# A graph-network kernel: one pipeline of node groups from the attention mix to the first maximum table, and ScalarE copies the carries

## The chip, the cores and the metric

The kernel runs on one core of a Trainium2 chip. The metric is the time of one execution in device microseconds (us), the median over runs. Engines are TensorE (PE in the rows, PEld for its weight loads), VectorE (DVE), ScalarE (ACT), GpSimd (POOL) and SyncE (SP), which here only issues DMAs.

## What is computed

Four graph layers over 6250 nodes of 96 features and 200,000 edges sorted by target node, each added to its input and normalised. The part around the change is the first layer and its two norms:

```
edge_index = stack([src, dst])
h = (x @ W).reshape(N, 4, 24)                       # attention, with a self loop per node
e = leaky_relu(a_src[src] + a_dst[dst], 0.2);  e = exp(e - segment_max(e, dst)[dst])
out = segment_sum(e / segment_sum(e)[dst] * h[src], dst) + gat_bias
proj = out @ proj_W.T + proj_b
z = x + proj
L0 = ln_g * norm(z) + ln_b                          # first norm
x = layernorm(x + L0)                               # second norm
x = layernorm(x + L1(x))                            # two maximum convolutions: segment_max(x[src] @ W_msg + edge_attr @ W_edge) ...
x = layernorm(x + L2(x));  x = layernorm(x + L3(x)) # two means, three GCN sums
```

## The kernel before

Nodes are padded to 49 blocks of 128, and handled in 7 groups (`NG`) of 7 blocks (`GB`). Edges lie in 128 partitions, each with a run of consecutive edges. The program is written by hand, engine by engine: each engine runs its own list of instructions in order, and semaphores (`wait_ge`, `then_inc`) are the only links. A group of rows is 128 x 672 numbers (7 blocks of 96), with the extra columns of attention 700 or 728.

The three passes over the edges (attention, and two maximum passes) are alike. GpSimd gathers the rows of the source nodes from a table in device memory (L449, one gather for 128 edges, a ring of 4 slots), VectorE scans them in place, ScalarE stores the running result to `hist`. When a pass is through, GpSimd gathers each node's last running result into `EG` (L506, 49 gathers, one semaphore `end_gathered[g]` a group). GpSimd then waits for all seven stores of the next table (`table_stored`) before it gathers for the next pass.

Behind the attention pass, which is where the change lies, the order before is:

1. **Carries.** What runs from one partition's edges into the next is worked out for each node: TensorE multiplies the selector matrix with the carry rows in three bf16 parts (L783, 21 products a group, in PSUM `psO`), VectorE copies a group to `CQ` (`ARENA`, L1596). One buffer, so that the two take turns, seven times. Then VectorE sets a bias row (L1223) and makes the self-loop logits.
2. **Mix and projection, group by group.** VectorE makes the logits' differences (L1745 to L1751), ScalarE their exponentials (L982), VectorE mixes three sources and divides (L1756 to L1760). TensorE transposes the seven blocks (L660), ScalarE copies them out with a bias (L884), TensorE multiplies by the projection and adds `X` through an identity product (L668 and L671, 14 products), ScalarE copies the result into `C` (L1027), VectorE takes its moments (`bn_stats`, L1176).
3. **First norm.** The statistics of all 49 blocks are finished together (`squares(slice(0, NB))`, one square root, `scales_of(slice(0, NB))`): no group is normalised before the last group has been projected.
4. **Second norm and first maximum table, group by group.** ScalarE normalises `C` (L1001), VectorE multiplies and adds into `X` and takes moments, ScalarE takes the square root (L995) and normalises `X` (L1001), TensorE transposes (L660) and multiplies (L668 with 192 columns), VectorE copies half to the table `TB` (`take_rows`, L1203) which SyncE stores, ScalarE the other half to `R` (L892).

ScalarE's functions come in table sets: exponential and square root are in different ones, and an `ACT_TABLE_LOAD` stands in its program where the set changes.

Of the kernel before, what the change touches and what calls it, by code (L numbers as in the profile page):

```python
# [83 lines left out]

def out_group_base(phase, kind):

    n = 0
    for f in range(9):
        if f == phase and kind == "rows":
            return n  # L90
        n += NG
# [7 lines left out]
def build(nc, x, src, dst, dst_before, src_tiles, dst_tiles, edge_attr, att_W, att_src, att_dst, gat_bias, proj_WT, proj_b, ln_g, ln_b,  # L99
# [176 lines left out]
    psM = [psA, psB, psX]  # L276
    step_sums = [psA[:, 0:CW], psB[:, 0:CW], psX[:, 512:512 + CW]]
# [86 lines left out]
    normed = sem("normed")  # L364
    sqrt_in = sem("sqrt_in")
# [277 lines left out]
    def _(pe):  # L643
        def node_phase(f):

            cols = PHASE_COLS[f]
            base = out_group_base(f, "rows")

            rowsrc = X if f in (ATT, MAX1, MEAN1, GCN1) else C if f in (PROJ, MAX2) else EGW
            bias = f in (PROJ, MAX1, MAX2, MEAN1, MEAN2)  # L650
# [12 lines left out]
            def multiply_group(g):  # L663

                pe.wait_ge(xt_copied, f * NG + g + 1)
                pe.wait_ge(out_used, g + (base + 1))
                for k in range(GB):
                    mm = pe.matmul(OUTG[:, k, 0:cols], XT[0:depth, g % 2, k * P:(k + 1) * P], WR[0:depth, f, 0:cols],  # L668
                                   start=True, stop=f != PROJ)
                    if f == PROJ:  # L670
                        mm = pe.matmul(OUTG[:, k, 0:cols], ident[:, :], X[:, g * GB + k, :], start=False, stop=True)  # L671
# [4 lines left out]
            if f == PROJ:  # L676
                for g in range(NG):
                    transpose_group(g)
                    multiply_group(g)
                return  # L680
            transpose_group(0)
            for g in range(NG):
                if g + 1 < NG:
                    transpose_group(g + 1)
                multiply_group(g)

# [72 lines left out]
        def carries(f, q):  # L759
# [17 lines left out]
            base = out_group_base(f, "carry")  # L777
            with pe.Fori(0, NG) as g:
# [70 lines left out]
        node_phase(PROJ)  # L849
        for f in (MAX1, MAX2, MEAN1, MEAN2, GCN1, GCN2, GCN3):  # L850
            q = PASS_OF_PHASE[f]
            node_phase(f)
# [24 lines left out]
    def _(act):  # L877
        def rows_transposed(f, g):

            act.wait_ge(transposed, f * NG + g + 1)  # L880
            if g >= 2:
                act.wait_ge(out_ready, out_group_base(f, "rows") + g - 1)
            if f == PROJ:
                nc.scalar.activation(XT[0:DIM, g % 2, :], psX[0:DIM, 0:GB * P], ACT.Identity,  # L884
                                     bias=gbT[:, 0:1]).then_inc(xt_copied, 1)
            else:
                nc.scalar.copy(XT[0:DIM, g % 2, :], psX[0:DIM, 0:GB * P]).then_inc(xt_copied, 1)
# [136 lines left out]
        def projected_rows(g):  # L1024

            act.wait_ge(out_ready, out_group_base(PROJ, "rows") + g + 1)
            nc.scalar.copy(C[:, g * GB:(g + 1) * GB, :], OUTG[:, :, 0:DIM]).then_inc(out_used, 1)  # L1027
# [5 lines left out]
        exp_of_group(0)  # L1033
        for g in range(NG):
            if g + 1 < NG:
                exp_of_group(g + 1)
            rows_transposed(PROJ, g)
            projected_rows(g)
# [4 lines left out]
        for g in range(NG + 2):  # L1043
            if g < NG:
                deviations(slice(g * GB, (g + 1) * GB))
            if g + 2 < NG:
                normalise(C, g + 2, normed)
            if g < NG:
                act.wait_ge(scales_known, g + 2)
                normalise(X, g, rows_ready)  # L1050
            if 1 <= g < NG + 1:
                rows_transposed(MAX1, g - 1)
            if g >= 2:
                root_rows(MAX1, g - 2)
# [33 lines left out]
    def _(dve):  # L1088
# [461 lines left out]
        def carries(f, q):  # L1550
# [28 lines left out]
            else:  # L1579
# [8 lines left out]
                small_sent()  # L1588
            start = steps[0]
            with dve.Fori(0, NG) as g:  # L1590
# [4 lines left out]
                if q == 0:  # L1595
                    link(ts(CQ[:, here, :], OUTG[:, :, 0:W0], 1.0, None, ALU.mult))  # L1596
                else:
                    link(tt(C[:, here, :], OUTG[:, :, 0:DIM],
                            cpen[:, here].unsqueeze(2).broadcast_to([P, GB, DIM]), ALU.add))
# [131 lines left out]
        def projected_halves(g):  # L1731

            dve.wait_ge(out_used, out_group_base(PROJ, "rows") + g + 2)
            for b in range(g * GB, (g + 1) * GB):
                step(halves_of(C, b))

        for r in range(RING):
            dve.wait_ge(hist_stored[r], 16 * LAPS)
        link(tt(zself[:, :, :], TB0[:, :, SW:W0], ADN[:, :, :], ALU.add))
        link(stt(zself[:, :, :], zself[:, :, :], 0.2, zself[:, :, :], ALU.mult, ALU.max))  # L1740
        link(tt(CQ[:, :, SW:W0], CQ[:, :, SW:W0], per(cpen[:, :], NB, HEADS), ALU.add))
        for g in range(NG):
            here = slice(g * GB, (g + 1) * GB)
            dve.wait_ge(end_gathered[g], 16 * GB)
# [7 lines left out]
            dve.sem_inc(exp_in, 1)  # L1752
            dve.wait_ge(exp_done, 2 * ITERS + 3 + g)
# [9 lines left out]
            dve.sem_inc(rows_ready, 1)  # L1763
            if g:
                projected_halves(g - 1)
        projected_halves(NG - 1)
        dve.wait_ge(dve_step, steps[0])
        squares(slice(0, NB))
        scales_of(slice(0, NB))
        for g in range(NG):  # L1770
# [4 lines left out]
            for b in range(g * GB, (g + 1) * GB):  # L1775
                step(halves_of(X, b))
            dve.wait_ge(dve_step, steps[0])
            squares(here)
            if g >= 3:
                take_rows(MAX1, g - 3)  # L1780
            scales_of(here)
        for g in range(NG - 3, NG):
            take_rows(MAX1, g)
# [70 lines left out]
```

## Time and profile before

| | before |
|---|---|
| median of 3 runs | 8222.67 us (8220.35 to 8223.56) |
| profiled execution | 8213.33 us, span of its instructions 8211.5 us |
| mean granted TensorE clock | 0.642 of full speed |
| busy over the span | PE 52%, DVE 67%, ACT 18%, POOL 60% |

The span is that of one profiled execution. Times in rows count from its start. The stretch that the change touches reaches from about 2184 to 2360 us.

### The profile page before, as it was taken

The numbers are of one execution on the slowest core, as the hardware profiler recorded it, in microseconds if no ns is written. First come the engines' busy times: TensorE is split into PE (matmuls) and PEld (weight loads), VectorE is DVE, ScalarE is ACT, GpSimd is POOL, SyncE is SP. The second block draws the span as 40 slices with busy tenths as digits, with TensorE's granted clock in tenths as the row PEclk, the third lists the DMA queues.
The fourth block names the chain that finished last, engine by engine and source line by source line (L and its number), as shares of the span: only waits on it lengthen the run. The fifth ranks groups of instructions, "written<-read, shape, count | busy, mean of one in ns | idle before, by whom it ended". The sixth has DMA issues, their size and how long they took to land.

```text
span 8211.5 us, 69615 instructions
## 1 busy us (share of the span) xinstructions
PE 4235.5 (52%) x19184; PEld 2465.7 (30%) x19184; DVE 5538.0 (67%) x13229; ACT 1494.4 (18%) x2140; POOL 4891.3 (60%) x5030
## 2 busy tenths in 40 slices
PE   2100000000155655656555555556565498999999
PEld 1000000000131111111113111111111298999999
DVE  4765555555578888888886888888888775222222
ACT  0222222222231121111111111111211200010000
POOL 6777777777637777777776777777777600000000
PEclk6555555555566565565655555565555599999999
DMA  5333333333224444444443444444444275766767
GB/s 145 86 93 86 85 86 85 86 85 86 66 86 130 129 129 132 131 130 130 129 130 103 129 130 132 130 130 129 130 131 131 80 263 201 267 225 227 268 220 247
DMA packets 642303, 1132.83 MB, mean 138 GB/s; under 512 B 164860, under 2 KB 422287, under 8 KB 641634
## 3 DMA queue, kind: packets, MB, share of 16 engines
q1 hardware_dynamic: 360256, 440.38, 16.7%
q0 software_dynamic: 159184, 251.10, 15.5%
q10 hardware_dynamic: 122578, 438.40, 13.4%
q14 instruction: 210, 1.72, 0.1%
q8 instruction: 75, 1.23, 0.1%
HBM read 716.67 MB, written 412.70 MB: 138 GB/s over the span
## 4 chain that ended last, share of the span: by engine, by line
POOL 57%; PE 20%; issue 18%; DVE 3%; ACT 1%; DMA 1%; DVEq 0%; POOLq 0%; ACTq 0%; SPq 0%
POOL CG L449 55%; PE psB L723 6%; PE psX L723 6%; PE psA L723 6%; PE psO L668 1%; POOL ad_starts L461 1%; POOL EG L506 1%; ACT X L1001 1%; POOL EG L441 0%; PE psX L660 0%; PE psO L783 0%; DVE BUF L1120 0%; DVE EG L1172 0%; PE psO L671 0%; DVE halves L1176 0%
## 5 line engine op out<-in xcount | busy, mean ns | idle before, releaser
L449 POOL DMA_INDIRECT CG<-table,BUF x4704 | 4532.5, 964 | 1564.2 <-issue 1432.1
L695 PE MATMUL psO<-WE,BUF 128*128 128x384 f32 x1568 | 1137.3, 880 | 106.8 <-DMA BUF<-in_edge_attr 99.8
L766 PE MATMUL psA<-ident,F 128*100 128x128 f32 x1 | 0.5, 452 | 1740.0 <-DVEq L1404 1740.0
L475 POOL CAST CG<-EG x35 | 26.9, 769 | 1297.9 <-DVEq L1173 1297.9
L953 ACT COPY psX<-BUF 128x384 f32<-128x384 f32 x392 | 189.0, 482 | 3210.7 <-DVE STG L1531 1618.2
L695 PEld LDWEIGHTS psO<-WE,BUF 128*128 128x128 f32 x1568 | 460.6, 324 | 619.4 <-DMA BUF<-in_edge_attr 371.6
L1429 DVE TENSOR_TENSOR terms<-CG,ARENA 128x32 f32<-128x32 f32 x196 | 45.1, 230 | 792.5 <-DMA CG<-table,BUF 792.0
L1493 DVE TENSOR_SCALAR BUF<-iota,EG 128x392 bf16<-128x392 f16 x1568 | 542.3, 346 | 0.0
L766 PEld LDWEIGHTS psA<-ident,F 128*100 128x100 f32 x1 | 0.2, 158 | 1740.3 <-DVEq L1404 1740.3
L702 PE MATMUL psB<-BUF 128*128 128x392 bf16 x523 | 251.2, 480 | 511.4 <-DVE BUF L1499 511.2
L702 PE MATMUL psA<-BUF 128*128 128x392 bf16 x523 | 252.1, 482 | 506.4 <-DVE BUF L1499 506.4
L723 PE MATMUL psA<-CG,BUF 128*128 128x288 bf16 x4018 | 509.9, 287 | 6.2 <-DMA BUF<-counts 6.2
L723 PE MATMUL psB<-CG,BUF 128*128 128x288 bf16 x4018 | 509.2, 287 | 7.1 <-DMA BUF<-counts 7.1
L702 PE MATMUL psX<-BUF 128*128 128x392 bf16 x522 | 251.4, 482 | 504.6 <-DVE BUF L1499 504.6
L1490 DVE TENSOR_SCALAR BUF<-iota,EG 128x128 bf16<-128x128 f16 x1568 | 496.4, 317 | 20.6 <-DMA EG<-step_rows 20.6
L723 PE MATMUL psX<-CG,BUF 128*128 128x288 bf16 x3969 | 500.8, 286 | 0.6 <-POOL CG L478 0.6
L723 PEld LDWEIGHTS psA<-CG,BUF 128*128 128x128 bf16 x4018 | 495.4, 142 | 9.5 <-POOL CG L478 6.7
L723 PEld LDWEIGHTS psB<-CG,BUF 128*128 128x128 bf16 x4018 | 495.1, 142 | 9.8 <-issue 7.5
L1499 DVE TENSOR_SCALAR BUF<-iota,EG 128x392 bf16<-128x392 f16 x1568 | 495.9, 316 | 0.0
L723 PEld LDWEIGHTS psX<-CG,BUF 128*128 128x128 bf16 x3969 | 488.3, 142 | 1.6 <-POOL CG L478 0.8
L1524 DVE TENSOR_TENSOR XTQ<-CG,psO 128x768 f32<-128x768 f32 x196 | 288.6, 1473 | 216.5 <-DMA CG<-table,BUF 216.3
L1524 DVE TENSOR_TENSOR STG<-CG,psO 128x768 f32<-128x768 f32 x196 | 288.8, 1473 | 207.4 <-DMA CG<-table,BUF 206.8
(279 smaller groups left out, 7912.3 us busy)
## 6 DMA issues: line engine op xcount, KB each, us to landing
BUF<-counts SPq DMA_DIRECT2D x245, 784.0 KB, 5.8
BUF<-counts ACTq DMA_DIRECT2D x245, 784.0 KB, 6.2
counts<-BUF SPq DMA_DIRECT2D x1572, 98.0 KB, 2.4
hist<-CG ACTq DMA_DIRECT2D x392, 384.0 KB, 2.5
hist<-CG ACTq DMA_DIRECT2D x196, 416.0 KB, 2.6
CG<-table,BUF POOLq DMA_INDIRECT x4704
BUF<-in_edge_attr SPq DMA_DIRECT2D x392, 128.0 KB
table<-TB SPq DMA_DIRECT2D x14, 336.0 KB, 2.6
```

The source lines that it names most:

```text
L449: pool.indirect_dma_start(out=rows_in[:, u % RING, k, :], out_offset=None, in_=tab, in_offset=bass.IndirectOffsetOnAxis(ap=SRC[:, u * S + ...
L461: pool.indirect_dma_start(out=ad_starts, out_offset=bass.IndirectOffsetOnAxis(ap=start_i[:, b:b + 1], axis=0), in_=ADN[:, b, :], in_offset ...
L506: pool.indirect_dma_start(out=EG[:, b * width:(b + 1) * width], out_offset=None, in_=rec, in_offset=bass.IndirectOffsetOnAxis(ap=last_i[:, ...
L668: mm = pe.matmul(OUTG[:, k, 0:cols], XT[0:depth, g % 2, k * P:(k + 1) * P], WR[0:depth, f, 0:cols], start=True, stop=f != PROJ)
L695: mm = pe.matmul(ETERM[:, s, a, 0:4 * DIM], EA[:, s, a, :], WE[:, m, :, :].rearrange("k c d -> k (c d)"), start=True, stop=True)
L702: pe.matmul(sums, LO[:, j, 0, :], RHS[:, j, 0, :], start=True, stop=False)
L723: mm = pe.matmul(sums[:, 0:3 * DIM], CNT16[:, B % 3, b:b + NB * (P - 1) + 1:NB], PARTS[:, b, :], start=b == 0, stop=b == NB - 1, skip_grou ...
L953: nc.scalar.copy(reset_cols[:, :, 1:K9], reset[:, u * S:(u + 1) * S].unsqueeze(1).broadcast_to([P, DIM // 2, S])).then_inc(resets_ready, 1)
L1490: ts(LO[:, j, 0, :], iota16[:, 0:P], STEP[:, 2, n:n + 1], None, ALU.is_equal)
L1493: ts(RHS[:, j, 0, :], iota16[:, :], STEP[:, 0, n:n + 1], None, ALU.is_equal)
L1499: ts(RHS[:, j, 1, :], iota16[:, :], STEP[:, 1, n:n + 1], None, ALU.is_equal).then_inc(onehot_ready, 1)
L1524: tt(max_cols[b][:, :, 1:K9].rearrange("p c (a k) -> p c a k", a=2), ROWSW[:, r, :, :].rearrange("p (a k) c -> p c a k", a=2), ETERM[:, s, ...
```

## The change

The carries are copied by ScalarE (`carried`), out of two PSUM buffers instead of one; four groups ahead of the pipeline and the other three within it. The node groups run through one loop of nine steps. In step `i` group `i` is mixed and projected, group `i-1` gets both its first norm and the addition into `X`, group `i-2` is normalised a second time and multiplied for the maximum table. The first norm's statistics are made group by group (`moments(C, i-1)`), so the wait for all seven groups is gone. The projection's products go to `psA` and `psB` and no longer share `psO`; ScalarE takes them out with two copies. The tables, semaphores and the passes before and behind are as they were.

```diff
+MIXED = [(f, g) for i in range(NG + 2) for f, g in ((MAX1, i - 2), (PROJ, i)) if g in range(NG)]
...
+        def mixed_phase():
+            base = out_group_base(MAX1, "rows")
+            for t, (f, g) in enumerate(MIXED):
+                pe.wait_ge(xt_copied, PROJ * NG + t)
+                if f == PROJ:
+                    pe.wait_ge(mixed_ready, g + 1)
+                else:
+                    pe.wait_ge(rows_ready, NG + g + 1)
+                for k in range(GB):
+                    mm = pe.transpose(psX[0:DIM, k * P:(k + 1) * P], (C if f == PROJ else X)[:, g * GB + k, :], ident[:, :])
+                mm.then_inc(transposed, 1)
+                pe.wait_ge(xt_copied, PROJ * NG + t + 1)
+                if f == PROJ:
+                    pe.wait_ge(proj_used, g)
+                    for k in range(GB):
+                        room = PROJ_OUT[k // 4][:, k % 4, :]
+                        pe.matmul(room, XT[:, t % 2, k * P:(k + 1) * P], WR[:, PROJ, 0:DIM], start=True, stop=False)
+                        mm = pe.matmul(room, ident[:, :], X[:, g * GB + k, :], start=False, stop=True)
+                    mm.then_inc(proj_ready, 1)
+                else:
+                    pe.wait_ge(out_used, g + (base + 1))
+                    for k in range(GB):
+                        mm = pe.matmul(OUTG[:, k, 0:2 * DIM], XT[:, t % 2, k * P:(k + 1) * P], WR[:, MAX1, 0:2 * DIM],
+                                       start=True, stop=True)
+                    mm.then_inc(out_ready, 1)
...
+            if q == 0:
+                for g in range(NG):
+                    pe.wait_ge(out_used, base + max(g, 1))
+                    for j in range(GB):
+                        for a in range(3):
+                            mm = pe.matmul(CARRY[:, g % 2, j, :], SEL16[:, (g * GB + j) * P:(g * GB + j + 1) * P],
+                                           Q_PARTS[:, a, :], start=a == 0, stop=a == 2)
+                    mm.then_inc(out_ready, 1)
+                return
...
-        deviations(slice(0, NB))
-        act.wait_ge(scales_known, 1)
-        normalise(C, 0, normed)
-        normalise(C, 1, normed)
...
+        EARLY_CARRIES = 4
+        for g in range(EARLY_CARRIES):
+            carried(g)
+        of_x = {}
+        for i in range(NG + 2):
+            if i < NG:
+                exp_of_group(i)
+            if i + EARLY_CARRIES < NG:
+                carried(i + EARLY_CARRIES)
+            if i >= 2:
+                act.wait_ge(scales_known, of_x[i - 2])
+                normalise(X, i - 2, rows_ready)
+            if 1 <= i <= NG:
+                of_c = group_deviations(i - 1)
+                act.wait_ge(scales_known, of_c)
+                normalise(C, i - 1, normed)
+            if i >= 2:
+                mixed_transposed(MAX1, i - 2)
+            if i < NG:
+                mixed_transposed(PROJ, i)
+                projected_rows(i)
+            if i >= 2:
+                root_rows(MAX1, i - 2)
+            if 1 <= i <= NG:
+                of_x[i - 1] = group_deviations(i - 1)
...
-        dve.wait_ge(dve_step, steps[0])
-        squares(slice(0, NB))
-        scales_of(slice(0, NB))
...
+        for i in range(NG + 2):
+            if i < NG:
+                shares(i)
+            if i >= 2:
+                scales_of(slice((i - 2) * GB, (i - 1) * GB))
+            if 1 <= i <= NG:
+                dve.wait_ge(proj_used, i)
+                moments(C, i - 1)
+                scales_of(slice((i - 1) * GB, i * GB))
+            if i < NG:
+                mixed_rows(i)
+            if i >= 2:
+                take_rows(MAX1, i - 2)
+            if 1 <= i <= NG:
+                first_norm_added(i - 1)
+                moments(X, i - 1)
```

The first place is ScalarE's list, behind the attention pass. Before, one group of the mix is three instructions (exponential, transposed rows, projected rows), seven times; this is the end of that loop and the first norm (`CG` holds `C` and the small arrays, `stat` the statistics, `XTQ` the transposed rows, `ARENA` holds `CQ` and `R`):

```order
L982 ACTIVATE CG<-CG 128x3x28
L884 ACTIVATE XTQ<-psX,gbT 96x896
L1027 COPY CG<-psO 128x672
L884 ACTIVATE XTQ<-psX,gbT 96x896
L1027 COPY CG<-psO 128x672
L995 ACT_TABLE_LOAD
L995 ACTIVATE stat<-stat,eps 128x49
L1001 ACTIVATE CG<-CG,stat 128x96 x14
```

Now, ScalarE's list in step 3 of the new loop, one of the five full steps:

```order
L1029 ACTIVATE stat<-stat,eps 128x7
L1016 ACT_TABLE_LOAD
L1016 ACTIVATE CG<-CG 128x3x28
L1035 ACTIVATE X<-X,stat 128x96 x7
L1029 ACT_TABLE_LOAD
L1029 ACTIVATE stat<-stat,eps 128x7
L1035 ACTIVATE CG<-CG,stat 128x96 x7
L1082 COPY XTQ<-psX 96x896
L1079 ACTIVATE XTQ<-psX,gbT 96x896
L1087 COPY CG<-psA 128x384
L1088 COPY CG<-psB 128x288
L926 COPY ARENA<-psO 128x672
```

The exponential of group `i` now stands between the square root of group `i-2` and that of group `i-1`. In the whole stretch ScalarE's program had one table load and has thirteen: seven ahead of square roots (L1029) and six ahead of exponentials (L1016).

The second place is TensorE's list at the same step (`psX` takes the transposes, `psO` the products for the table, `psA` and `psB` the projection):

```order
L698 MATMUL psX<-ident,X 96x128 x7
L711 MATMUL psO<-WR,XTQ 128x192 x7
L698 MATMUL psX<-ident,CG 96x128 x7
L705 MATMUL psA<-WR,XTQ 128x96
L706 MATMUL psA<-X,ident 128x96
L705 MATMUL psA<-WR,XTQ 128x96
```

The projection of group `i` stands behind the table products of group `i-2`. Before, all seven projections stood ahead of the first table product.

## Rows read from the trace of the kernel before

**Rows 1.** The page's costliest group: busy us, mean ns, idle before and its releaser.

```profile
L449 POOL DMA_INDIRECT CG<-table,BUF x4704 | 4532.5, 964 | 1564.2 <-issue 1432.1
```

**Rows 2.** Timeline of GpSimd: start us, us, engine, line, operation, [idle before <-releaser].

```profile
2166.51 0.94 POOL L449 DMA_INDIRECT CG<-table,BUF  x1 [0.30 <-issue]
2183.88 0.94 POOL L506 DMA_INDIRECT EG<-hist,last_i  x1 [16.42 <-DMA hist<-CG]
...
2192.75 0.94 POOL L506 DMA_INDIRECT EG<-hist,last_i  x1 [0.30 <-issue]
...
2360.06 0.94 POOL L449 DMA_INDIRECT CG<-table,BUF  x1 [108.76 <-DMA table<-TB]
```

**Rows 3.** Windows: stretch, PE, PEld, DVE, ACT, POOL busy us (count), PEclk, DMA, GB/s.

```profile
2187.00:2212.00 25.00, 13.99 (x147) 12.45 (x147) 6.42 (x7) 0.00 (x0) 18.91 (x21) 0.50 0.21 42
2212.00:2295.00 83.00, 53.94 (x245) 50.55 (x245) 56.74 (x137) 13.42 (x21) 31.08 (x28) 0.56 0.09 19
...
2310.00:2357.00 47.00, 29.64 (x147) 26.47 (x147) 26.29 (x84) 36.73 (x92) 0.00 (x0) 0.80 0.16 45
```

**Rows 4.** Timeline: a gathered slot's first use, the first carries, the first shares.

```profile
2169.07 0.21 DVE L1429 TENSOR_TENSOR terms<-CG,ARENA 128x32 f32<-128x32 f32 x1 [4.39 <-DMA CG<-table,BUF]
...
2187.19 2.00 PE L783 MATMUL psO<-SCR,SEL 128*128 128x104 bf16 x21 [2.15 <-DVEq L1404]
2189.46 0.92 DVE L1596 TENSOR_SCALAR ARENA<-psO 128x728 f32 x1 [2.82 <-PE psO L783]
...
2215.02 0.19 DVE L1745 TENSOR_TENSOR EG<-EG,vpen 128x28 f32<-128x28 f32 x1
```

**Rows 5.** Timeline of one group in the mix and projection.

```profile
2256.26 0.27 ACT L982 ACTIVATE CG<-CG 128x84 f32<-128x84 f32 x1 [2.54 <-DVEq L1752]
2256.44 0.99 ACT L884 ACTIVATE XTQ<-psX,gbT 96x896 f32<-96x896 f32 x1
2256.57 0.89 DVE L1756 TENSOR_TENSOR EG<-EG,CG 128x700 f32<-128x700 f32 x1 [0.40 <-ACT CG L982]
...
2257.48 0.74 PE L668 MATMUL psO<-WR,XTQ 97*128 97x96 f32 x2 [3.25 <-ACT XTQ L884]
...
2261.54 0.86 DVE L1760 TENSOR_TENSOR CG<-EG,CG 128x672 f32<-128x672 f32 x1
...
2263.56 1.70 PE L660 MATMUL psX<-ident,CG 128*96 128x128 f32 x7
2263.80 0.72 ACT L1027 COPY CG<-psO 128x672 f32<-128x672 f32 x1 [6.38 <-PE psO L671]
```

**Rows 6.** Timeline: the first norm's table load, then moments and root of a group.

```profile
2295.01 1.28 ACT L995 ACT_TABLE_LOAD   x1
...
2297.43 0.34 ACT L995 ACTIVATE stat<-stat,eps 128x49 f32<-128x49 f32 x1 [1.13 <-DVEq L1184]
...
2303.03 1.22 DVE L1176 BATCH_NORM_STATS2 halves<-X 128x6 f32<-128x96 f32 x7
...
2305.15 0.30 ACT L995 ACTIVATE stat<-stat,eps 128x7 f32<-128x7 f32 x1 [1.44 <-DVEq L1184]
```

**Rows 7.** Timeline of the second norm and the maximum table.

```profile
2318.09 4.43 PE L668 MATMUL psO<-WR,XTQ 97*128 97x192 f32 x14
...
2322.60 0.94 PE L660 MATMUL psX<-ident,X 128*96 128x128 f32 x7
...
2324.31 2.51 PE L668 MATMUL psO<-WR,XTQ 97*128 97x192 f32 x14 [0.77 <-ACT ARENA L892]
...
2326.77 2.60 ACT L1001 ACTIVATE X<-X,stat 128x96 f32<-128x96 f32 x7
...
2356.05 0.86 DVE L1203 TENSOR_SCALAR TB<-psO 128x672 f32<-128x672 f32 x1 [3.45 <-PE psO L668]
```

**Rows 8.** Timeline: a change of table set with nothing to wait for.

```profile
211.85 1.28 ACT L927 ACT_TABLE_LOAD   x1
213.15 0.23 ACT L927 ACTIVATE EX<-EX 128x36 f32<-128x36 f32 x1
```

More of the change, by code:

```diff
@@ L1022, in _, with carried @@
         exp(QT[:, 3, :])
-        def projected_rows(g):
-            act.wait_ge(out_ready, out_group_base(PROJ, "rows") + g + 1)
-            nc.scalar.copy(C[:, g * GB:(g + 1) * GB, :], OUTG[:, :, 0:DIM]).then_inc(out_used, 1)
+        def carried(g):
+            base = out_group_base(ATT, "carry")
+            act.wait_ge(out_ready, base + g + 1)
+            nc.scalar.copy(CQ[:, g * GB:(g + 1) * GB, :], CARRY[:, g % 2, :, :]).then_inc(out_used, 1)
         def exp_of_group(g):
             exp(E3[:, :, g * GB:(g + 1) * GB, :])
-        exp_of_group(0)
@@ L1034, in _, with mixed_transposed @@
[L1034 to L1038, printed above, removed]
-        deviations(slice(0, NB))
-        act.wait_ge(scales_known, 1)
-        normalise(C, 0, normed)
-        normalise(C, 1, normed)
[L1043 to L1054, printed above, removed]
+        def mixed_transposed(f, g):
+            t = MIXED.index((f, g))
+            act.wait_ge(transposed, PROJ * NG + t + 1)
+            if t >= 2:
+                f2, g2 = MIXED[t - 2]
+                if f2 == PROJ:
+                    act.wait_ge(proj_ready, g2 + 1)
+                else:
+                    act.wait_ge(out_ready, out_group_base(MAX1, "rows") + g2 + 1)
+            if f == PROJ:
+                nc.scalar.activation(XT[0:DIM, t % 2, :], psX[0:DIM, 0:GB * P], ACT.Identity,
+                                     bias=gbT[:, 0:1]).then_inc(xt_copied, 1)
+            else:
+                nc.scalar.copy(XT[0:DIM, t % 2, :], psX[0:DIM, 0:GB * P]).then_inc(xt_copied, 1)
@@ new lines, in projected_rows, with group_deviations @@
+        def projected_rows(g):
+            act.wait_ge(proj_ready, g + 1)
+            nc.scalar.copy(C[:, g * GB:g * GB + 4, :], PROJ_OUT[0])
+            nc.scalar.copy(C[:, g * GB + 4:(g + 1) * GB, :], PROJ_OUT[1]).then_inc(proj_used, 1)
+        def group_deviations(g):
+            deviations(slice(g * GB, (g + 1) * GB))
+            return roots[0] - 1
+        EARLY_CARRIES = 4
[23 more added lines that the diff above has]
+                of_x[i - 1] = group_deviations(i - 1)
@@ L1594, in carries @@
                 dve.sem_inc(turn["dve"], 1)
[L1595 to L1599, printed above, removed]
+                link(tt(C[:, here, :], OUTG[:, :, 0:DIM],
+                        cpen[:, here].unsqueeze(2).broadcast_to([P, GB, DIM]), ALU.add))
                 dve.sem_inc(out_used, 1)
@@ L1729, in _, with shares @@
         bias_row()
[L1731 to L1742, printed above, removed]
+        def shares(g):
             here = slice(g * GB, (g + 1) * GB)
+            dve.wait_ge(out_used, out_group_base(ATT, "carry") + g + 2)
+            link(tt(CQ[:, here, SW:W0], CQ[:, here, SW:W0], per(cpen[:, here], GB, HEADS), ALU.add))
             dve.wait_ge(end_gathered[g], 16 * GB)
@@ L1752, in _, with mixed_rows @@
             dve.sem_inc(exp_in, 1)
+        def mixed_rows(g):
+            here = slice(g * GB, (g + 1) * GB)
             dve.wait_ge(exp_done, 2 * ITERS + 3 + g)
@@ L1762, in _, with moments, first_norm_added @@
                     rden[:, here, :].unsqueeze(3).broadcast_to([P, GB, HEADS, HDIM]), ALU.mult))
[L1763 to L1766, printed above, removed]
-        dve.wait_ge(dve_step, steps[0])
-        squares(slice(0, NB))
-        scales_of(slice(0, NB))
-        for g in range(NG):
+            dve.sem_inc(mixed_ready, 1)
+        def moments(V, g):
+            for b in range(g * GB, (g + 1) * GB):
+                step(halves_of(V, b))
+            dve.wait_ge(dve_step, steps[0])
+            squares(slice(g * GB, (g + 1) * GB))
+        def first_norm_added(g):
             here = slice(g * GB, (g + 1) * GB)
@@ L1774, in _ @@
             link(tt(X[:, here, :], X[:, here, :], C[:, here, :], ALU.add))
[L1775 to L1783, printed above, removed]
+        for r in range(RING):
+            dve.wait_ge(hist_stored[r], 16 * LAPS)
+        link(tt(zself[:, :, :], TB0[:, :, SW:W0], ADN[:, :, :], ALU.add))
+        link(stt(zself[:, :, :], zself[:, :, :], 0.2, zself[:, :, :], ALU.mult, ALU.max))
+        dve.sem_inc(rows_ready, NG)
+        for i in range(NG + 2):
[14 more added lines that the diff above has]
+                moments(X, i - 1)
         rows_taken(MAX1)
```

33 lines of the change are left out of this document (15 added, 18 removed).

## The prediction, made before the changed kernel ran

> **What bounds the kernel now.** I read the page's costliest groups first: 4704 gathers by GpSimd take 4532.5 us, and its idle time ahead of them is nearly all issue, 0.3 us a gather [rows 1]. So in the three edge passes GpSimd is the bound, and what lies between two passes counts in full: it ends when GpSimd may gather again. GpSimd's timeline gives that stretch: the last gather of the attention pass at 2166.51, the first of each node's last result at 2183.88, the first of the next pass at 2360.06, after 108.76 us of waiting for the table's stores [rows 2]. VectorE takes the last table rows at 2356.05 to 2356.91 [rows 7]; 3.15 us later GpSimd starts. The question is only when this last take comes in the new order.
>
> Before, the stretch has three parts. The carries take turns, PE 2.0 us and VectorE 0.9 us [rows 4], seven times, and the first shares start at 2215.02 [rows 4]. Then come seven groups of mix and projection, with PE busy 53.9 of 83 us and ScalarE only 13.4 [rows 3]. Then the barrier and the second loop, in which ScalarE is busy 36.7 of 47 us [rows 3]. The clock granted to PE averages 0.56 in the second part and 0.80 in the last [rows 3]: mostly the 1.2 GHz level there, mostly 2.4 GHz here.
>
> **The change part by part.** I lay the new lists behind each other, each instruction starting when its engine and its inputs are free, 0.05 to 0.1 us for a handoff (L884 ends at 2257.43 and PE starts at 2257.48 [rows 5]).
>
> *Start.* The carries no longer hold VectorE. Its first shares then need the seven gathers of group 0: the seventh is issued at 2192.75 and takes 0.94 us [rows 2]; the same gather in the pass ends issuing at 2167.45 [rows 2] and is used at 2169.07 [rows 4], 1.6 us for landing. So shares start near 2195.3, 19.7 us earlier. ScalarE copying 728 columns costs about 0.78 (0.72 for 672 [rows 5], by size) and hides under PE's 2.0 a group; the three late copies add some 0.7 each, one of them to a full step. GpSimd's later groups of gathers come every 9 us, faster than steps consume them.
>
> *Front, steps 0 and 1.* Shares 1.3 (six operations of 0.19 with gaps [rows 4]), exponential 0.4, mix 5.9 (2256.57 to 2262.40 [rows 5]), transposes 1.7, copy 1.0 [rows 5], projection 6.3 (2257.48 to 2263.80 [rows 5]), two copies 0.85: 17.7 with handoffs, and group 1 waits for all of it, since its moments of `C` stand ahead of its mix. Then moments 2.1 (2303.03 to 2305.15), root 0.4 [rows 6] and two small operations 0.45, mix 5.9, transposes to copies 9.9: 18.8. Together 36.5.
>
> *Five full steps (2 to 6).* Here the chain runs down ScalarE's list, with PE's work in its middle: root of `X` 0.2, **table load 1.28**, exponential 0.2, normalising `X` 2.5, **table load 1.28**, root of `C` 0.3, VectorE's scales 0.5, normalising `C` 2.5, copy 0.9, table products 4.4, transposes 1.7, copy 1.0, projection 6.3, two copies 0.75, root rows 0.6 [rows 5 to 7]: 24.4, and ten handoffs 0.5, makes 24.9 at the 1.2 GHz level. The waits added on ScalarE, for the projection above all, hold the root rows and the root of `X` behind them, and VectorE's scales wait for that root; this is why I let the chain run through them. VectorE's mix (5.9) lies beside the normalising, copy and products (7.8), its adding and moments (3.9) beside the projection; neither is on the chain. PE has 14.1 us of work in such a step, ScalarE about 12.
>
> The load needs no input, so ScalarE does it as soon as it stands first. At 211.85 one starts, and the exponential behind it at 213.15: 1.3 us for the whole change [rows 8]; I take the load's 1.28. The other end comes from the barrier, where the load starts at 2295.01 and the root at 2297.43 [rows 6]: 2.4 us, though there the root also waited for VectorE. The Trainium skill (ScalarE: Activation LUTs, What ACT_TABLE_LOAD costs) gives some 2.66 us for a change of set, 1.28 for the load and 1.38 for a drain, and tells the reader to group functions by set; by it the ten loads in full steps would cost 13.8 us more, the sum 24 us instead of 10.5. No drain is seen ahead of the exponential in this trace [rows 8].
>
> *Clock.* In the second loop the table products took 4.43 us at one level and 2.51 at the other, transposes 1.7 and 0.94 [rows 7, 5]; the projection products at the upper level are not in the trace, and by the same ratio would take 3.6. In the new step PE idles about 6 us behind a projection and 4 behind the transposes of `X`, so I take the table products at 4.4. They run into the transposes of `C` without a gap, and such a stretch is what stood ahead of the rise near 2322 (4.43, then 0.94 [rows 7]); the projection follows after 1.1 us. So I take transposes and projection at the upper level: 24.9 - 0.8 - 2.7 = **21.4 a step**, five steps 107. The bounds are 24.9 (never raised) and, with 1.9 less for the products, 19.5 (always).
>
> *Tail.* After step 6 group 5's `X` and group 6's `C` are still to go, and group 6's whole second norm: scales 0.5, normalise 2.5, root and scales 0.8, normalise 2.5, copy 0.9, products 4.4, take 0.9, add 1.8, moments 2.1, root and scales 0.8, normalise 2.6, transposes 1.7, copy 1.0, products 4.4, take 0.9: with handoffs 28.6.
>
> *Sum.* 2195.3 + 36.5 + 107 + 28.6 = 2367.4, against 2356.9: **10.5 us later**. The 19.7 us won at the start and the barrier's wait are spent on steps that each hold both norms, both transposes and both products in one chain: before, a group cost 10.8 us in the mix loop and 6 to 7 in the other. SyncE's stores stand in no other order, nothing is moved past them, and the next pass follows as before; the ring of four slots (32 gathers, 40 us) covers the wait of VectorE for its step tables, which moves along.
>
> The profiled execution took 8213.33 us, so it would take 8223.8; the median of the runs shown is 9.3 us above it, so I set the same 10.5 on 8222.67: **8233 us**. A measurement of this kernel can tell about 0.2%, 16.4 us, from no change; this is below that.
>
> **The rivals.**
>
> *The clock stays at 1.2 GHz* in the new loop: PE's share of a step is 14.1 of 24.9 us, less than the 53.9 of 83 that got 0.56 [rows 3]. Then 5 x 24.9 = 124.5, the end is 2384.9, and the kernel is 28 us slower: **8251 us**, slower. It decides for "slower" from 22.6 us a step on. Against it: the products with 192 columns are the densest work, and they are followed at once by transposes.
>
> *A change of set costs up to 2.4 us*, the time between load and root at the barrier [rows 6], as the engine must run empty first: 1.1 us more for each of ten loads in full steps and some 2 us outside them give 13 more, **8246 us**, slower. The exponential at 213.15 [rows 8] speaks against it. The Trainium skill (ScalarE: Activation LUTs, What ACT_TABLE_LOAD costs) states such a drain.
>
> *PE runs at the upper level throughout* (from 2336 to 2357 it did nearly so before, with gaps of 2 us): front 29.6, steps 19.5, tail 24.5 give 2346.9, 10 us earlier: **8212.7**, still within 0.2%.
>
> *Loads hidden besides*: if ScalarE's two loads a step both fell in waits, 2.6 us a step go, and with the upper clock the time is 8200, faster. But in the list the load stands behind a root or normalising on which the chain itself runs, so only front and tail hide theirs.
>
> *The change does nothing to the path*: if the start were bound by the gathers as late as the carries were, the end would move by the steps alone. The gathers' rows exclude that: group 0 is complete 20 us before 2215.
>
> **How the numbers follow.** The forecast (clock up for part of each step, loads 1.3) 0.60; clock mostly down 0.17; dearer loads or handoffs 0.10; clock up throughout 0.10; that and hidden loads 0.03. Within the forecast, half a microsecond a step more or less is 2.5 us, and where in the step the clock rises is 4 us, so its own range is 8226 to 8241, of which a sixth lies beyond 8239. Slower: 0.17 + 0.10 + a tenth from the forecast, less what of the two rivals stays below 16.4: 0.32. Same: 0.64. Faster: 0.04. The range takes the forecast, most of both slower rivals and half of the upper clock: 8215 to 8249.
>
> **What would show it.** Right: shares of group 0 near 2195; thirteen table loads of 1.28 us, with the instruction behind starting at once; full steps of about 21 us, with PE idle twice and ScalarE waiting for the projection; last take near 2367; the next pass 3 us later. Wrong: steps of 25 (clock), of 24 with idle time behind each load (drain), of 19 (clock up), or a start later than 2200. If the steps come out as worked and the total does not, something behind the first maximum table moved, for which I see no reason.

## The result, and the profile after

| | before | after |
|---|---|---|
| median | 8221.73 us (8218.61 to 8228.09, 22 runs) | 8233.79 us (8226.26 to 8242.68, 22 runs) |
| ratio | | 1.0013, 95% interval 1.0008 to 1.0019 |
| span, profiled execution | 8211.5 us | 8227.6 us (execution 8229.37) |
| stretch: first end gather to GpSimd's next pass | 176.18 us | 188.06 us |
| first shares, from the first end gather | 31.1 us | 11.5 us |
| end of the last take | 173.0 us | 184.9 us |

"First shares" is VectorE's first instruction of the mix (the logits' differences of group 0), "last take" its copy of the last table rows (`take_rows`), and an "end gather" one of GpSimd's 49 gathers of last results.

By the ratio the change costs 0.13%, 10.7 us (6.6 to 15.6 by the interval); the two medians lie 12.1 us apart. The forecast was 8233 us, 10.5 us later, and within the 0.2% that was called "same". The profiled spans differ by 16.1 us; 4.1 of it lies ahead of the change, since the first end gather starts at 2188.01 and not at 2183.88 [rows 2]. That part is scatter between executions: in the experiments below this gather starts anywhere from 2182.84 to 2190.66, on the ordinary chips. The stretch takes the other 11.9. The page names the same costliest group as before [rows 1]:

```profile
L457 POOL DMA_INDIRECT CG<-table,BUF x4704 | 4541.0, 965 | 1576.8 <-issue 1432.7
```

GpSimd's timeline of after, against [rows 2]:

```profile
2188.01 0.95 POOL L514 DMA_INDIRECT EG<-hist,last_i  x1 [16.45 <-DMA hist<-CG]
...
2205.11 1.53 POOL L514 DMA_INDIRECT EG<-hist,last_i  x1 [0.31 <-issue]
...
2376.07 0.95 POOL L457 DMA_INDIRECT CG<-table,BUF  x1 [120.83 <-DMA table<-TB]
```

VectorE's timeline, first shares (against [rows 4]) and last take (against [rows 7]):

```profile
2199.54 0.19 DVE L1801 TENSOR_TENSOR EG<-EG,vpen 128x28 f32<-128x28 f32 x1 [5.54 <-DMA EG<-hist,last_i]
...
2372.07 0.86 DVE L1268 TENSOR_SCALAR TB<-psO 128x672 f32<-128x672 f32 x1 [10.43 <-PE psO L711]
```

The shares no longer follow the carries. They wait for gathered rows, and at the other end VectorE waits 10.43 us for the last group's products and what stands ahead of them. The windows of after (columns as in [rows 3]) are roughly front, five full steps, tail:

```profile
2196.00:2233.00 37.00, 18.42 (x152) 16.93 (x149) 20.87 (x60) 10.27 (x19) 28.76 (x28) 0.59 0.19 40
2233.00:2340.00 107.00, 53.39 (x272) 48.33 (x271) 66.74 (x199) 58.29 (x120) 17.36 (x17) 0.66 0.10 25
2340.00:2372.00 32.00, 15.45 (x64) 13.39 (x62) 9.04 (x42) 12.34 (x30) 0.00 (x0) 0.61 0.05 14
```

In the steps no engine is full: PE half, ScalarE 58 of 107 us, VectorE 67. That fits a chain that goes from engine to engine. One full step on ScalarE shows its links:

```profile
2236.04 0.31 ACT L1029 ACTIVATE stat<-stat,eps 128x7 f32<-128x7 f32 x1
2236.37 1.28 ACT L1016 ACT_TABLE_LOAD   x1
2237.67 0.27 ACT L1016 ACTIVATE CG<-CG 128x84 f32<-128x84 f32 x1
2237.85 0.75 ACT L1062 COPY ARENA<-psO 128x728 f32<-128x728 f32 x1
2238.49 2.61 ACT L1035 ACTIVATE X<-X,stat 128x96 f32<-128x96 f32 x7
2241.12 1.28 ACT L1029 ACT_TABLE_LOAD   x1
2242.42 0.30 ACT L1029 ACTIVATE stat<-stat,eps 128x7 f32<-128x7 f32 x1
2243.24 2.61 ACT L1035 ACTIVATE CG<-CG,stat 128x96 f32<-128x96 f32 x7 [0.53 <-DVEq L1257]
2245.76 0.88 ACT L1082 COPY XTQ<-psX 96x896 f32<-96x896 f32 x1
2252.31 1.00 ACT L1079 ACTIVATE XTQ<-psX,gbT 96x896 f32<-96x896 f32 x1 [5.66 <-PE psX L698]
2256.77 0.48 ACT L1087 COPY CG<-psA 128x384 f32<-128x384 f32 x1 [3.45 <-PE psB L706]
2257.14 0.41 ACT L1088 COPY CG<-psB 128x288 f32<-128x288 f32 x1
2257.43 0.74 ACT L926 COPY ARENA<-psO 128x672 f32<-128x672 f32 x1
2258.04 0.32 ACT L1029 ACTIVATE stat<-stat,eps 128x7 f32<-128x7 f32 x1
```

From 2236.04 to 2258.04 the step takes 22.0 us. ScalarE waits twice, 5.66 us for the transposes of `C` and 3.45 for the projection. The same step on TensorE:

```profile
2241.25 1.70 PE L698 MATMUL psX<-ident,X 128*96 128x128 f32 x7 [5.91 <-ACT X L1035]
2246.70 4.81 PE L711 MATMUL psO<-WR,XTQ 97*128 97x192 f32 x14 [3.75 <-ACT XTQ L1082]
2251.34 0.93 PE L698 MATMUL psX<-ident,CG 128*96 128x128 f32 x7
2253.36 0.46 PE L705 MATMUL psA<-WR,XTQ 97*128 97x96 f32 x2 [1.09 <-ACT XTQ L1079]
```

It idles 5.91 and 3.75 us, does the transposes of `X` and the table products at the clock's lower level, 1.2 GHz (1.70 and 4.81 us, against 0.94 and 2.51 at the upper one, 2.4 GHz [rows 7]), and then the transposes of `C` at the upper one (0.93).

### The profile page after: what moved, and what is told of

Its sections match the earlier page's. It is cut to its first block, busy times and chain, and to the rows that moved or that the text cites. A ratio compares the mean times of both kernels' runs of the same rounds, so it can differ in the third digit from the quotient of the medians.

```text
span 8227.6 us, 69574 instructions
## 1 busy us (share of the span) xinstructions
PE 4233.3 (51%) x19184; PEld 2457.8 (30%) x19184; DVE 5535.2 (67%) x13264; ACT 1515.7 (18%) x2170; POOL 4899.9 (60%) x5030
## 3 DMA queue, kind: packets, MB, share of 16 engines
q8 instruction: 76, 1.25, 0.1%
## 4 chain that ended last, share of the span: by engine, by line
POOL 57%; PE 19%; issue 18%; DVE 3%; ACT 2%; DMA 1%; DVEq 0%; POOLq 0%; ACTq 0%; SPq 0%
POOL CG L457 55%; PE psX L751 6%; PE psB L751 6%; PE psA L751 6%; PE psO L676 1%; POOL ad_starts L469 1%; POOL EG L514 1%; ACT X L1035 1%; POOL EG L449 1%; PE psO L711 0%; DVE EG L1237 0%; DVE BUF L1185 0%; PE psX L668 0%; DVE CG L1236 0%; DVE TB L1265 0%
## 5 line engine op out<-in xcount | busy, mean ns | idle before, releaser
L1555 DVE TENSOR_SCALAR BUF<-iota,EG 128x128 bf16<-128x128 f16 x1568 | 495.3, 316 | 19.5 <-DMA EG<-step_rows 19.5
```

The source lines that it names most:

```text
L1555: ts(LO[:, j, 0, :], iota16[:, 0:P], STEP[:, 2, n:n + 1], None, ALU.is_equal)
```

## The experiments

Times in the trace are counted from the first end gather. Ratios are to the kernel before, run on the same chip. The first four kernels ran on a chip where the kernel before took 9733.68 us (9642 to 9789), 18% more. In experiment 1's trace of that chip nearly all of it lies in waits of GpSimd: 2965.6 us ahead of its gathers in place of 1564.2 [rows 1], 1369.3 of them for the stores of `hist`. They ran again on other chips with a before near 8210 to 8225 us, and those runs decide.

**1. The carries alone.** The kernel before, with the carries as the change has them and the rest of it as before:

```diff
+                            mm = pe.matmul(CARRY[:, g % 2, j, :], SEL16[:, (g * GB + j) * P:(g * GB + j + 1) * P],
+                                           Q_PARTS[:, a, :], start=a == 0, stop=a == 2)
...
+            nc.scalar.copy(CQ[:, g * GB:(g + 1) * GB, :], CARRY[:, g % 2, :, :]).then_inc(out_used, 1)
...
-        link(tt(CQ[:, :, SW:W0], CQ[:, :, SW:W0], per(cpen[:, :], NB, HEADS), ALU.add))
+            link(tt(CQ[:, here, SW:W0], CQ[:, here, SW:W0], per(cpen[:, here], GB, HEADS), ALU.add))
```

> The kernel before with one part of the change: ScalarE copies the carries out of two PSUM buffers, four groups ahead of the mix and three behind the first exponential; the two loops and the barrier at the first norm stay. Stretch means from GpSimd's first gather of last results to its first gather of the next pass, 176.2 us before and 188.1 us in the changed kernel. Theory (start and steps are separate terms): first shares 11.4 us behind the stretch's start instead of 31.1, the rest as before plus 1.2 us for seven small operations instead of one, so a stretch of 157.5 to 158 us and 8203 to 8205 us in all, ratio 0.998, faster than both kernels. Rival (the early start is lost because gathers of the last results then hold the mix, or because it was hidden): stretch 170 us or more, less than 7 us gained.

Measured: 9665.16 us, ratio 0.9935 (0.9906 to 0.9964), but not with the stretch expected: 219.11 us, because the second shares came at 77.8 us. TensorE's timeline there:

```profile
2439.97 5.03 PE L784 MATMUL psO<-SCR,SEL 128*128 128x104 bf16 x63 [1.71 <-DVEq L1424]
2448.42 1.40 PE L784 MATMUL psO<-SCR,SEL 128*128 128x104 bf16 x14 [3.42 <-issue]
2450.45 0.25 PE L784 MATMUL psO<-SCR,SEL 128*128 128x104 bf16 x1 [0.63 <-issue]
2451.84 0.25 PE L784 MATMUL psO<-SCR,SEL 128*128 128x104 bf16 x1 [1.14 <-issue]
```

Behind the first 77, most of the carry products come one by one, "issue" ahead of each, while GpSimd gathers (its last end gather starts at 2498.39, the last of the single products at 2505.18). No trace of the kernel before exists on that chip, so where this run won its 0.65% is not known. On an ordinary chip:

> The kernel before with ScalarE's carries alone, once more, because on the chip of its first run every pass was 18% longer and TensorE stood still for 56 us between the first and the second shares while GpSimd gathered. Stretch: from GpSimd's first gather of last results to its first of the next pass. Theory (the start is worth 19.7 us less 1.2 for small operations, and the stall belongs to that chip): where the kernel before takes 8220 us, first shares at 11.5 us, second near 20, stretch 157.5 to 158, 18 us gained, ratio 0.998. Rival (the products of the carries, written out 147 times instead of looped, are held up wherever GpSimd gathers): the second shares at 30 us or later, less than 10 us gained.

Measured: 8192.94 us, ratio 0.9978 (0.9969 to 0.9988), stretch 155.82 us, shares at 11.5, 21.7, 32.8 us. No stall:

```profile
2185.71 8.50 PE L784 MATMUL psO<-SCR,SEL 128*128 128x104 bf16 x126 [1.71 <-DVEq L1424]
```

So this half of the change is worth 20.4 us of the stretch, 19.6 of it at the start.

**2. The pipeline alone.** The changed kernel with VectorE's carries in one buffer:

```diff
-        for g in range(EARLY_CARRIES):
-            carried(g)
...
+                if q == 0:
+                    link(ts(CQ[:, here, :], OUTG[:, :, 0:W0], 1.0, None, ALU.mult))
```

> The changed kernel with the other part alone: VectorE copies the carries as before, one buffer, ahead of everything; the nine-step loop stays. Theory: the start goes back by 19.7 us and the three late copies leave ScalarE's list, of which at most 1.5 us was on the chain: stretch 206 to 208 us, 30 us slower than before, ratio 1.0037. Rival (the pipeline is held by gathers or by something late in the stretch, so that its start does not matter): stretch 195 us or less.

Measured: 9725.15 us, ratio 1.0017 (0.9989 to 1.0046), with the first shares at 87.4 us; it tells nothing of the pipeline. The stall is there too, but in another place. TensorE did its third 21 products from 2456.14 to 2458.14 without a gap, and VectorE's copy of them started 47 us later:

```profile
2456.14 2.00 PE L811 MATMUL psO<-SCR,SEL 128*128 128x104 bf16 x21 [10.77 <-issue]
...
2505.33 0.92 DVE L1648 TENSOR_SCALAR ARENA<-psO 128x728 f32 x1 [49.54 <-remote]
```

Again on an ordinary chip:

> The changed kernel, with the carries copied by VectorE in one buffer as before, all seven ahead of the first shares; the rest of the pipeline stays. Theory (the pipeline itself lengthens the stretch from the first end gather to the first gather of the next pass, and only the carries' move takes some back): the first shares start 31 to 32 us after the first end gather, 20 us later than in the changed kernel, and everything behind them keeps its length, so the stretch is 206 to 208 us against 188.1 in the changed kernel and 176.2 before, and the kernel is 30 us (ratio 1.0037) slower than before. Rival (the late start hides in the pipeline, since later groups wait for something else): a stretch of 195 us or less, ratio below 1.0025.

Measured: 8256.0 us, ratio 1.0041 (1.0027 to 1.0055). First shares at 31.1 us as before, stretch 210.10 us: 34 more than before, 22 more than after (theory: 18 to 20; behind the shares it takes 179.0 us where after takes 176.5, with a granted clock of 0.59 for 0.63). The late start hides nowhere. The 2 to 4 us beyond the theory stand in the third full step, the only one in which the projection came at the lower level:

```profile
2298.54 0.32 ACT L1020 ACTIVATE stat<-stat,eps 128x7 f32<-128x7 f32 x1
...
2322.30 0.48 ACT L1078 COPY CG<-psA 128x384 f32<-128x384 f32 x1 [6.38 <-PE psB L706]
...
2323.58 0.32 ACT L1020 ACTIVATE stat<-stat,eps 128x7 f32<-128x7 f32 x1
```

It takes 25.04 us; the other four take 21.0 to 21.9.

**3. No change of table set.** The exponential of the shares is replaced by a function of the square root's set that writes 1; this leaves that part of the computation out:

```diff
-            exp(E3[:, :, g * GB:(g + 1) * GB, :])
+            nc.scalar.activation(part, part, ACT.Identity, bias=ones[:, 0:1], scale=0.0).then_inc(exp_done, 1)
```

> The changed kernel with the exponential of the three shares replaced by a constant 1 made by a function of every table set, so that only one table load is left in the stretch; the attention weights are left out of the result. Theory (both loads of a full step are on the chain): a step falls from 21.5 to 18.9 or 19.5 us, the stretch from 188 to between 175 and 179 us, about the length of before. Rival (the loads fall into waits for PE or VectorE): stretch within 2 us of 188. Second rival (a change of set costs 2.7 us with its drain): a fall of 24 us or more, to 164 us or less.

Measured: 9739.44 us, ratio 1.0019 (0.9986 to 1.0053); the stall again. From the third shares on it takes 11.0 us less than after: its five full steps take 18.7 to 20.0 us, 19.3 on average. On an ordinary chip:

> The changed kernel without any change of table set in its loop (the exponential of the shares is replaced by a constant 1, so the attention weights are left out), once more beside the others. Theory: full steps of 19 to 19.5 us instead of 21.5, stretch 176 to 179 us instead of 188.1. Rival (loads hidden): 186 or more.

Measured: 8210.05 us, ratio 0.9999 (0.9990 to 1.0009), stretch 180.35 us, 7.7 less than after and 1.4 above the range. Its steps are 19.0, 19.6, 22.7, 19.0 and 19.7 us: four of them some 2.2 us below after's mean of 21.5, and one above it, in which the projection came at the lower level:

```profile
2292.61 0.48 ACT L1090 COPY CG<-psA 128x384 f32<-128x384 f32 x1 [6.38 <-PE psB L706]
```

The ten loads in full steps are on the chain, and at no more than their own 1.28 us each (2.2 us a step for two of them, in this run and in the one before it); the slower projection took back a third of what those steps gained (5 x 2.2 = 11.0 us, and 7.7 was left).

**4. The second norm earlier.** ScalarE's list in another order, the root and normalising of `X` at the end of their own step:

```diff
-            if i >= 2:
-                act.wait_ge(scales_known, of_x[i - 2])
-                normalise(X, i - 2, rows_ready)
...
+            if 1 <= i <= NG:
+                of_x = group_deviations(i - 1)
+            if i + 1 < NG and i:
+                exp_of_group(i + 1)
+            if 1 <= i <= NG:
+                act.wait_ge(scales_known, of_x)
+                normalise(X, i - 1, rows_ready)
```

> The changed kernel with another order on ScalarE alone: in each step the root of X, the next exponential with both its table loads and the normalising of X stand ahead of the copies of the projection instead of behind them, so that they run while PE multiplies the projection. Theory (a full step is one chain through ScalarE and PE, 21.5 us, of which PE is two waits): about 4 us of ScalarE's work goes beside the projection's 3.4 us, but PE then goes up and down in another rhythm; stretch 178 to 182 us. Rival (PE with its clock is the bound and the order on ScalarE is not): stretch 186 to 189 us.

Measured: 9724.15 us, ratio 0.9980 (0.9948 to 1.0012): not told apart from no change. On an ordinary chip:

> The changed kernel with another order in ScalarE's list: the root and the normalising of X stand at the end of a step, behind the copies of the projection, and the exponential of the next group ahead of them, so that the second norm of a group no longer waits for the next step. Theory (the chain runs down ScalarE's list, and what counts is what stands behind its wait for the projection): some 1 us a step less, a stretch of 178 to 184 us against 188.1. Rival (the order only moves the waits, the step keeps its sum of work): 186 to 189 us.

Measured: 8227.75 us, ratio 1.0004 (0.9994 to 1.0014), stretch 185.10 us, 3 less than after: between the two. The transposes of `X` now come at the start of a step, but TensorE then waits 5.76 us for `XTQ` and runs the products at the lower level:

```profile
2239.56 4.85 PE L711 MATMUL psO<-WR,XTQ 97*128 97x192 f32 x14 [5.76 <-ACT XTQ L1082]
2244.20 1.70 PE L698 MATMUL psX<-ident,CG 128*96 128x128 f32 x7
```

**5. The clock held.** Unneeded transposes of the identity fill TensorE's two waits of a step in the changed kernel, 24 and 12, then 40 and 26:

```diff
+                if f == MAX1:
+                    held(24, psX[:, 7 * P:8 * P])
...
+                if f == MAX1:
+                    pe.wait_ge(proj_used, min(g + 2, NG))
+                    held(12, psA[:, 0:P])
```

> The changed kernel with transposes of the identity, whose results nobody reads, put into TensorE's two waits of each step (24 ahead of the transposes of X, 12 ahead of the table products). Theory (table products run at 1.2 GHz because TensorE has been idle for 6 and 4 us before them): the granted clock in the loop rises from 0.66 to over 0.9, table products take 2.5 us instead of 4.8, a full step 19.5 us instead of 21.5, stretch 176 to 180 us. Rival (the added transposes delay TensorE's own work, or the clock is not what holds a step): stretch 187 us or more.

Measured: 8216.34 us, ratio 1.0007 (0.9997 to 1.0017), stretch 183.59 us. Behind the filler of 24 transposes 3.25 us of waiting were left in four of the five full steps, and the table products still took 3.7 to 4.9 us in all five. Hence the longer filler:

> The changed kernel with 40 and 26 unneeded transposes of the identity in TensorE's two waits of each step, in place of 24 and 12 in the run before, in which the table products still took 3.6 to 4.9 us each and the stretch 183.6. Theory (the gap of 3 us left behind the filler let the clock fall): with the gaps filled the table products take 2.5 us in each step, a step 19.5 us or less, the stretch 175 to 179 us. Rival (the level is not held by filling, or the filler itself delays TensorE's next work): table products above 3.5 us or late starts, and a stretch of 183 us or more.

Measured: 8217.86 us, ratio 0.9994 (0.9984 to 1.0004), stretch 179.22 us, 8.8 less than after; the granted clock over the stretch is 0.83 (0.63 after). The first steps are as the theory has them:

```profile
2252.25 4.53 PE L694 MATMUL psX<-ident 128*128 128x128 f32 x40
2258.28 0.94 PE L705 MATMUL psX<-ident,X 128*96 128x128 f32 x7 [1.50 <-ACT X L1045]
2259.06 3.00 PE L694 MATMUL psA<-ident 128*128 128x128 f32 x26
2263.74 2.54 PE L721 MATMUL psO<-WR,XTQ 97*128 97x192 f32 x14 [1.67 <-ACT XTQ L1092]
2266.37 0.94 PE L705 MATMUL psX<-ident,CG 128*96 128x128 f32 x7
```

That step takes 19.35 us. In three later ones the products take 3.3 to 3.6 us and the step 20.6 to 20.8. So the lower level accounted for some 2 us a step. With the clock up in much of the full steps and the tail the stretch is still 3 us above before. The filler did not reach the front, whose two projections stayed at 6.38 us each, 2.9 us more than at the upper level, so this does not show what the pipeline would take with the clock up throughout.

**6. The moments later, on top of experiment 1.** In the old mix loop VectorE's moments of `C` for group g stood ahead of the mix of group g+2, and waited for its projection. They move one group back:

```diff
-            if g:
-                projected_halves(g - 1)
+            if g >= 2:
+                projected_halves(g - 2)
+        projected_halves(NG - 2)
```

> The kernel before with ScalarE's carries, and besides with VectorE's moments of C taken two groups behind the mix instead of one, barrier and both loops as before. Theory (in the mix loop VectorE waits 2.2 us a group for the projection of the group before): groups of 9.3 to 9.6 us instead of 10.8, 7 to 9 us less than with the carries alone, stretch 149 to 152 us and 8195 to 8198 us in all where the kernel before takes 8222. Rival (TensorE's 8 us a group at 1.2 GHz with its two handoffs is the bound): groups stay at 10.3 us or more, stretch within 3 us of 158.

Measured: 8189.6 us, ratio 0.9974 (0.9963 to 0.9984), stretch 155.08 us where 149 to 152 was expected. The groups follow every 10.0 us in place of 11.0, but no faster, for this reason on VectorE's timeline:

```profile
2246.51 0.19 DVE L1765 TENSOR_TENSOR EG<-EG,vpen 128x28 f32<-128x28 f32 x1 [0.99 <-DMA EG<-hist,last_i]
```

GpSimd's end gathers have become the bound of the loop; the last of the 49 starts at 69.08 us, the last shares at 71.6. The barrier behind the loop came only 1.9 us earlier. To see whether it is the gathers or TensorE's low clock, filler of 8 and 24 transposes a group went into the same kernel's mix loop:

> The fastest version so far (the kernel before with carries by ScalarE in two buffers and the moments of C taken two groups behind; stretch 155.1 us, groups of the mix every 10.0 us), with 8 and 24 unneeded transposes of the identity a group in TensorE's waits of the mix loop. Theory A (the low clock in TensorE's share of the mix loop is the bound): groups every 9.0 us and a stretch of some 149 us. Theory B (what I favour by the trace of the run before, in which the shares of a group wait some 1 us for its gathered rows): GpSimd's end gathers set the 10 us a group, and only the last group and the barrier gain: a stretch of 152 to 155 us, within 3 us of the run before.

Measured: 8199.88 us with 8224.6 for before on its chip, ratio 0.9972 (0.9961 to 0.9983), stretch 152.70 us, clock 0.80 over it. The shares stay 10 us apart and wait as before:

```profile
2242.25 0.19 DVE L1771 TENSOR_TENSOR EG<-EG,vpen 128x28 f32<-128x28 f32 x1 [1.13 <-DMA EG<-hist,last_i]
```

Theory B: the gathers are the bound, and the clock is worth 2.4 us behind them. The intervals of this kernel and of the one without filler overlap; by its ratio to before either is faster than both kernels of the case.

## Why the prediction was right

| step | predicted | measured |
|---|---|---|
| first shares, from the first end gather | 11.4 us | 11.5 |
| front, steps 0 and 1, to the root of `X` | 36.5 | 36.5 |
| five full steps | 107 (21.4 each) | 107.7 (22.0, 20.9, 22.1, 21.6, 21.0) |
| tail, to the end of the last take | 28.6 | 29.2 |
| last take against before | +10.5 | +11.9 |
| take to GpSimd's next pass | 3.15 | 3.14 |

*Start.* Right, and shown by experiments 1 and 2 from both sides: with the carries' move alone the shares come at 11.5 us, without it at 31.1, and the end moves by as much or more.

*Full steps, the chain through ScalarE's list.* Right. The links stand in the rows above in the predicted order. Experiment 4 shows that the order on ScalarE does matter, though little: what it saves at one wait is mostly spent at another.

*Table loads.* The size was right, 1.30 us from the load's start to the next function in each of the full steps (2236.37 to 2237.67, 2241.12 to 2242.42), and so was the choice against the Trainium skill (ScalarE: Activation LUTs, What ACT_TABLE_LOAD costs): this trace does not agree with its 2.66 us for a switch, and no drain stands ahead of any of the loads. Experiment 3 bears out that they lie on the chain. One number was wrong: the prediction and the section on the change speak of thirteen loads, seven and six; the trace has eleven, six ahead of roots and five ahead of exponentials, since the exponentials of the first two steps follow no root, and the roots of the last two follow roots. The sum had used ten in full steps, which is what there is, so it did not suffer.

*Clock.* Right in kind: in all five steps the projection came at the upper level (ScalarE's wait for it 3.45 us, against 6.38 in the front), the table products at the lower. Their cost was 4.4 to 4.85 us where 4.4 was taken, and in the third and fourth step the transposes of `C` took 1.70 and 1.15 us in part or in whole at the lower level; these and, in the first step, a late carry's copy of 0.75 us make the slower steps. In the tail the two table products took 4.85 us each where 4.4 was taken. Both bounds of the clock were met: with the clock up a step took 19.35 us (experiment 5, predicted 19.5), and the one full step of experiment 2 with its projection at the lower level took 25.04 (predicted 24.9). Such a step costs some 3.5 us more. One of five came in each of experiment 2's two traces and one in the second trace of experiment 3, none in the profiled execution of after. That all five projections were at the upper level there is in part luck, and what decides it was not tried.

*The rivals.* "The clock stays at 1.2 GHz" is excluded by the rows, "a change of set costs up to 2.4 us" by the eleven loads and by experiment 3. "The upper level throughout" was not the case, but experiment 5 came near it: stretch -8.8 us against after, where the rival, with front and tail at the upper level too, had the end 20.5 us below the forecast; of that, the filler reached only the full steps and the tail. Luck is in the agreement of the medians, 8233 and 8233.79 us: the last take came 1.4 us later than predicted, and the median of before, on which the forecast stood, was 0.9 us lower in the longer series.

*What the change was made of.* Its two halves have opposite signs: -20.4 us for the carries, and 34 us more for the pipeline when alone, 32.2 on top of the carries (188.06 less 155.82). The pipeline removed a barrier and lost. From the first shares to the end of the last take its front, five full steps and tail take 36.5 + 107.7 + 29.2 us, 173.4 in all, where the two loops with the barrier between them took 141.9. A full step brings one group through both halves of the work in some 21.5 us; the two loops did it in 10.7 and some 6.5 us a group, and the barrier was waited for once. Of the 4.3 us between them the table loads are 2.2 (experiment 3).

## What to carry to other kernels

Count a removed barrier against the length of one pipelined step: where stages of several groups take turns in one engine's ordered list, the step is the sum of their links, not the longest engine's work. Where a change has two halves, cost and try each alone; here the first half alone is 0.22% faster than before, and with the moments moved 0.26%. A table load that stands between two links cost about its own duration here each time (1.1 of 1.28 us by experiment 3), so functions are best kept in groups by set, or the change of set put beside a wait.

## What was not expected of the hardware

- On the chip where everything took 18% longer, TensorE issued most of the carry products singly in experiment 1, 0.25 us of work every 0.7 to 1.4 us at first, while GpSimd gathered at 1.25 us each; the second shares came 56 us late. On an ordinary chip the first 126 products took 8.50 us without a gap. In experiment 2 the products came in whole groups, and VectorE's copies were late instead, by 11.91 and 49.54 us of waiting; so a stall also comes without the single issue and without the written-out list of products. In both traces it ends within some 10 us of GpSimd's last end gather. Whether instruction fetch, the gathers or the memory is behind it stays open, as no kernel was made for it.
- Filling waits with transposes held TensorE's upper level only in part. With 3.25 us left of the wait ahead of the transposes of `X`, the table products behind took 3.7 us and more; with 1.4 to 1.7 us left in both waits, 2.54 in some steps and 3.3 to 3.6 in others. What decides between the two was not tried.
- Some of GpSimd's end gathers took 1.53 us and not 0.95, without any wait shown (the one at 2205.11 in GpSimd's timeline of after). Beside that one VectorE ran its mix:

```profile
2204.94 0.89 DVE L1818 TENSOR_TENSOR EG<-EG,TB 128x700 f32<-128x700 f32 x1
2205.86 0.33 DVE L1819 RECIPROCAL CG<-EG 128x28 f32<-128x28 f32 x1
2206.23 0.86 DVE L1820 TENSOR_TENSOR CG<-EG,CG 128x672 f32<-128x672 f32 x1
```

The ten end gathers of after that took longer than 1 us, and the fourteen of experiment 6, all lie beside VectorE's operations on two inputs of 672 or 700 columns, by 0.77 us or more each; those away from them took 0.94 to 0.96 us. Some beside them took no longer either, and no kernel was made to part the two, so the cause is argued, not shown. In experiment 6 seven gathers took 10.0 us in place of 8.75 and set the pace of the mix loop, so that VectorE's mix may itself slow the gathers that it then waits for.
